# Decoder kernel with four attentions: a second bank for part of the causal stage's key projection, and GpSimd's stacking of head pairs cut in two around an addition

## Chip, cores and metric

One core of one Trainium2 chip. The metric is the device time of one execution in microseconds (us); of several executions the median is given.

## What is computed

A post-norm decoder of two layers on x of 4 x 512 x 512, float32. Each of six blocks is added to its input and layer-normalised:

```python
x = _layernorm(x + _L0_attn_ref(x, ...), axis=-1)        # rope attention, 4 heads of 128
x = _layernorm(x + _L0_xattn_ref(x, ctx, ctx, gamma))    # 8 heads over channels, below
x = _layernorm(x + _L0_ffn_ref(x, ...), axis=-1)         # ternary weights, Hadamard
x = _layernorm(x + _L1_attn_ref(x, ...), axis=-1)        # causal, 16 heads of 32, below
x = _layernorm(x + _L1_xattn_ref(x, ctx, mask), axis=-1)
x = _layernorm(x + _L1_ffn_ref(x, ...), axis=-1)         # 4-bit weights
# _L0_xattn: q, k, v are reshaped to (B, 8, 64, 512)
qk = jnp.einsum('bhdq,bhdl->bhql', qh, kh) * scale
ret = gamma * jnp.einsum('bhql,bhdl->bhdq', softmax(qk), vh)
# _L1_attn
kqv = (x @ Wqkv + bqkv).reshape(b, s, 3, 16, 32)
scores = jnp.einsum('bsnh,btnh->bnst', k, q) / math.sqrt(32)   # then masked to be causal
out = jnp.einsum('bnkq,bknh->bqnh', softmax(scores), v).reshape(b, s, 512) @ Wo + bo
```

Products that need more than one pass of float32r are split: each operand is kept as a high part and the rest, a low part, and the products high x high, high x low and low x high are summed.

## The kernel before

The program is written by hand, engine by engine. Each stage is a function (`head_attention` is the second, `causal_attention` the fourth) with one block per engine; the order inside a block is fixed by loops, and semaphores tie the blocks together. PSUM has eight banks of 128 x 512 float32, and all stages share them by number.

**Second attention** (`head_attention`, L708 on). The work is 16 groups g, one for two heads (a pair) of one batch, each of 8 tiles k (two heads, four tiles of queries). On TensorE a step makes the scores of a tile (L911, two matmuls, banks 0 to 2), transposes the probabilities of the tile three steps back (L80), and at k = 4 and 6 works off the previous group: values (L941), and at k = 6 also the inverse sums spread over partitions (L955). VectorE takes the maximum of each tile (L860), ScalarE the exponential (L829). At k = 1 of group g + 2 VectorE scales the output of group g (L880).

The operands of the scores are stacked by `HeadPairs`. SyncE loads a group's x and context into one of two slots (`load`), once the stack that used the slot is done. GpSimd then runs `stack` (L693): high part of the context (L696), scaled x (L697), high part of x (L699), then low part of the context (L701) and the low part of x (L704), which counts `stacked`. TensorE waits for `stacked` before the first scores of a group, so before k = 0. GpSimd's loop is

```python
for g in range(PAIRS):
    if g + 2 < PAIRS:
        stack(g + 2)          # waits scores_ready of group g first
    if g == 0:
        past.norm.root(pool, B - 1)
    norm.root(pool, 0, g - 2)
    add(g)                    # waits scaled (L880 of group g), adds into X (L800)
```

so the addition of group g stands behind the stack of group g + 2 and before that of group g + 3. `past.norm.root` (L164) belongs to the first attention's last batch; `norm.root` (L197, L199) to this stage's.

**Causal attention** (`causal_attention`, L1640 on). 16 groups G (four heads of one batch each; NF = 4 groups a batch) of 11 steps k. While group G's scores (L2057), transposes (L2068), values (L2088), tail (L2095) and spread (L2108) run, `project` (L2021) makes queries and keys of group G + 1: queries (j = 0) at steps 0, 0 and 1, keys (j = 1) at steps 3, 3 and 4, three passes of four matmuls each. Both use bank 6. ScalarE keeps the high part (`first.high`, L1155) and VectorE the low part (`first.low`, L1159, which counts `qk_low`) one step after the last pass. Before the first pass of the keys TensorE waits for `qk_low` of the queries, since they share the bank. Bank 7 holds the spread inverse sums (steps 7 to 8 of each group), and in some groups a transposed x, a value projection or an output.

## Time and profile before

| | |
|---|---|
| time, median of 3 runs | 1730.44 us (1727.53 to 1731.41) |
| profiled execution: its time | 1730.36 us |
| profiled execution: its span | 1728.6 us |
| TensorE busy | 1586.3 us (92%) |
| VectorE busy | 1273.3 us (74%) |
| ScalarE busy | 945.9 us (55%) |
| GpSimd busy | 734.0 us (42%) |
| second attention, on TensorE | from 259 to 482 us |
| causal attention, on TensorE | from 818 to 1260 us, about |

The profile comes from one execution. PE is TensorE's matmul side and PEld its weight load, DVE is VectorE, ACT ScalarE, POOL GpSimd, SP SyncE. L with a number is a line of the kernel; a helper's line stands for all who call it. In a timeline row stand the start and the duration in us, and in brackets how long the engine had been idle before it and what released it. Where a wait is for several semaphores the one named can be one that had long been there, and then it was another, often a transfer. The granted clock is TensorE's: 1.00 is its higher level of 2.4 GHz, 0.50 the lower of 1.2 GHz.

### The profile page before, as it was taken

What the parts mean: (1) busy time and instruction counts of PE and PEld (TensorE: products, weight loads), DVE (VectorE), ACT (ScalarE), POOL (GpSimd) and SP (SyncE); (2) the same over time, 40 slices, a digit from 0 to 9 for tenths busy, and PEclk for the clock granted to TensorE, in tenths of its full rate; (3) what the DMA queues carried; (4) which work ended last, traced back from release to release, by engine and by line L of the source; (5) the groups of instructions that cost most, each with busy time, mean ns of one, the idle gap of its engine ahead of it and who ended that gap; (6) DMA issues with size and microseconds to landing.
All of it is one profiled execution on the core that took longest, in us unless ns stands there. A gap on an engine that the chain in (4) does not pass through costs nothing. (4 is left out here: it accounts for less than half of the span.)

```text
span 1728.6 us, 26389 instructions
## 1 busy us (share of the span) xinstructions
PE 1586.3 (92%) x8780; PEld 1116.2 (65%) x8812; DVE 1273.3 (74%) x2261; ACT 945.9 (55%) x1945; POOL 734.0 (42%) x707
## 2 busy tenths in 40 slices
PE   8999998999866999998999999899898988999995
PEld 5778875566524566666667566566566766777774
DVE  6466656766878899997686684875759999767574
ACT  3222226886666676766575474663634555555642
POOL 5044164777631444534432232231233245556563
PEclk9999999999988999999999999999899999999998
DMA  6200018533020000004221121221233100000000
GB/s 219 74 1 25 1 49 214 182 118 102 23 98 1 1 1 1 1 1 125 76 74 53 55 74 38 56 74 37 88 107 94 49 1 1 1 25 25 1 25 25
DMA packets 66850, 95.73 MB, mean 55 GB/s; under 512 B 12176, under 2 KB 28688, under 8 KB 66716
## 3 DMA queue, kind: packets, MB, share of 16 engines
q1 hardware_dynamic: 60044, 81.18, 15.4%
q0 software_dynamic: 6144, 12.60, 2.8%
q8 instruction: 72, 1.18, 0.3%
q14 instruction: 62, 0.51, 0.1%
q10 hardware_dynamic: 528, 0.26, 0.1%
HBM read 56.25 MB, written 4.19 MB: 35 GB/s over the span
## 5 line engine op out<-in xcount | busy, mean ns | idle before, releaser
L2996 PE MATMUL bank<-fp_xT,fp_weights_values 128*128 128x512 f32 x704 | 187.4, 405 | 11.0 <-DVE fp_gate L2899 9.4
L1827 ACT ACTIVATE causal_probs<-bank,causal_neg 128x512 f32<-128x512 f32 (+3 forms) x256 | 134.5, 532 | 99.8 <-DVE causal_neg L1897 65.8
L2996 PEld LDWEIGHTS bank<-fp_xT,fp_weights_values 128*128 128x128 f32 x704 | 129.8, 190 | 56.6 <-DVE fp_gate L2899 17.4
L3023 PE MATMUL bank<-fp_wd,fp_hT 128*128 128x512 f32 x528 | 133.7, 394 | 4.6 <-DVE X L2921 3.5
L2908 DVE SCALAR_TENSOR_TENSOR fp_up<-bank,fp_weights_scales,fp_up 128x512 f32<-128x512 f32 x132 | 99.1, 751 | 43.9 <-ACT fp_up L2806 36.8
L860 DVE TENSOR_REDUCE heads_neg<-bank 128x1 f32<-128x512 f32 x128 | 86.5, 678 | 55.6 <-PE bank L911 55.6
L3023 PEld LDWEIGHTS bank<-fp_wd,fp_hT 128*128 128x128 f32 x528 | 98.5, 188 | 29.0 <-issue 6.6
L829 ACT ACTIVATE heads_probs<-bank,heads_neg 128x512 f32<-128x512 f32 x128 | 88.5, 696 | 42.8 <-DVE heads_neg L860 42.8
L1552 PE MATMUL bank<-weights_raw,ternary_qT 128*128 128x512 bf16 x433 | 104.7, 387 | 6.9 <-DVE ternary_z L1420 5.0
L1226 POOL TENSOR_TENSOR ternary_z<-ternary_z 128x1024 f32<-128x1024 f32 x16 | 37.7, 2357 | 165.4 <-DVE ternary_z L1420 165.4
L1167 POOL DMA_DIRECT2D causal_qS<-causal_qk x96 | 48.9, 516 | 135.3 <-DVE causal_qk L1159 135.2
L2068 PE MATMUL bank<-eye,causal_probs 128*128 128x128 f32 x640 | 100.2, 280 | 5.6 <-ACT causal_pT L1809 3.7
L355 POOL TENSOR_TENSOR rope_qk<-rope_rot 128x512 f32<-128x512 f32 x32 | 43.0, 1344 | 143.3 <-DVE rope_rot L458 141.8
L2779 POOL TENSOR_TENSOR fp_gate<-fp_gate 128x512 f32<-128x512 f32 x44 | 57.0, 1295 | 100.4 <-DVE fp_gate L2899 100.4
L2057 PE MATMUL bank<-causal_kS,causal_qS 96*128 96x512 f32 (+3 forms) x256 | 84.1, 380 | 16.9 <-ACT causal_probs L1827 13.9
L2800 ACT ACTIVATE fp_gate<-bank,fp_weights_scales 128x512 f32<-128x512 f32 x88 | 60.1, 688 | 61.5 <-PE bank L2996 55.6
L92 PE MATMUL bank<-rope_xT,rope_wT 128*128 128x512 f32 x372 | 90.2, 398 | 2.0 <-DVE rope_wT L445 2.0
L2068 PEld LDWEIGHTS bank<-eye,causal_probs 128*128 128x128 f32 x640 | 76.2, 143 | 24.1 <-issue 14.6
L2899 DVE SCALAR_TENSOR_TENSOR fp_gate<-bank,fp_weights_scales,fp_gate 128x512 f32<-128x512 f32 x88 | 63.8, 747 | 30.0 <-ACT fp_gate L2800 29.5
L92 PEld LDWEIGHTS bank<-rope_xT,rope_wT 128*128 128x128 f32 x372 | 68.9, 188 | 20.1 <-DVE rope_wT L445 4.3
L394 ACT ACTIVATE rope_qkT<-rope_qk 128x512 fp32r<-128x512 f32 x32 | 20.3, 634 | 112.2 <-POOL rope_qk L355 112.2
L1552 PEld LDWEIGHTS bank<-weights_raw,ternary_qT 128*128 128x128 bf16 x448 | 44.2, 100 | 56.6 <-DVE ternary_z L1420 7.5
(268 smaller groups left out, 4233.3 us busy)
## 6 DMA issues: line engine op xcount, KB each, us to landing
pairs_xd<-X SPq DMA_DIRECT2D x64, 128.0 KB, 2.6
pairs_cd<-in_ctx SPq DMA_DIRECT2D x64, 128.0 KB, 2.8
causal_qS<-causal_qk SPq DMA_DIRECT2D x96, 64.0 KB, 2.8
causal_qS<-causal_qk POOLq DMA_DIRECT2D x96, 64.0 KB, 2.5
causal_kS<-causal_qk SPq DMA_DIRECT2D x96, 64.0 KB, 2.9
causal_kS<-causal_qk POOLq DMA_DIRECT2D x96, 64.0 KB, 2.6
X<-in_x SPq DMA_DIRECT2D x4, 1024.0 KB, 7.9
heads_cT<-in_ctxT SPq DMA_DIRECT2D x4, 1024.0 KB, 6.0
```

Source lines behind the costliest of these rows:

```text
L92: last = pe.matmul(bank, lhs(a, k), rhs(c, k), start=n == 0, stop=n == len(steps) - 1)
L829: act.activation(probs[:, n % 4], banks[n % 3][:], ACT.Exp, bias=neg[:, g % 2, k:k + 1], accum_out=total[:, g % 2, k:k + 1]).then_inc(prob ...
L860: dve.tensor_reduce(neg[:, g % 2, k:k + 1], banks[n % 3][:], AX, ALU.max, negate=True).then_inc(neg_ready, 1)
L1552: last = pe.matmul(to[:], qT[:, t % 2, k], w[c][:, k], start=k == 0, stop=k == NF - 1)
L1827: act.activation(probs_of(i)[:, h + one], view[:, one], ACT.Exp, bias=neg[:, G % 2, at:at + 1], accum_out=total[:, G % 2, at:at + 1]).then ...
L2057: last = pe.matmul(view[:, one], qS[0:3 * DH, G % 2, h + one, i * P:(i + 1) * P], kS[0:3 * DH, G % 2, h + one, 0:(i + 1) * P], start=True, ...
L2068: last = pe.transpose(banks[3 + n % 2][:, h * P:(h + 1) * P], probs_of(i)[:, h, j * P:(j + 1) * P], ident)
L2800: act.activation(gate[:, n % 2, g // 2], banks[4 + g][:], ACT.Copy, scale=scale(n, g, 0)).then_inc(gate_even, 1)
L2899: dve.scalar_tensor_tensor(out=part, in0=banks[4 + g][:], scalar=scale(n, g, 0), in1=part, op0=ALU.mult, op1=ALU.add).then_inc(gate_odd, 1)
L2908: dve.scalar_tensor_tensor(out=up[:, n % 2], in0=banks[4 + g][:], scalar=scale(n, g, 1), in1=up[:, n % 2], op0=ALU.mult, op1=ALU.add).then ...
L2996: last = pe.matmul(banks[4 + g][:], values[:, g, n % NI, of], xT[:, part, g], start=part == 0, stop=part == 1)
L3023: last = pe.matmul(banks[t][:], hT[:, n % SLOTS, a, t * P:(t + 1) * P], wd[:, c, i], start=i == 0 and k == 0, stop=i == NI - 1 and k == 2)
```

## The change

Two parts that share no code.

1. `HeadPairs.stack` is cut into `highs` (three operations) and `lows` (two), and GpSimd's loop in the second attention becomes: `highs` of group g + 2, addition of group g - 1, `lows` of group g + 2, root. The addition is one iteration older. In the first iteration the root of the first attention's last batch stands between the halves.
2. In the causal attention the keys of a group G with G % 4 of 0 or 1 are projected into bank 7. There TensorE waits for `spread_kept` of group G - 3 instead of `qk_low` of the same group's queries. The spread of a group (L2108 before) waits for `qk_low` of all keys projected up to then.

```diff
     def stack(self, pool, g):
-        xd, cd, xS, cH, cL = (tile[:, g % 2] for tile in (self.xd, self.cd, self.xS, self.cH, self.cL))
+        self.highs(pool, g)
+        self.lows(pool, g)
+
+    def highs(self, pool, g):
+        xd, cd, xS, cH = (tile[:, g % 2] for tile in (self.xd, self.cd, self.xS, self.cH))
         pool.wait_ge(self.loaded[g % 2], 128 * (g // 2 + 1))
         pool.tensor_scalar(cH, cd, 1.0, 1.0, ALU.mult, ALU.mult).then_inc(self.high_c, 1)
         pool.tensor_scalar(xd, xd, self.SCALE, 1.0, ALU.mult, ALU.mult).then_inc(self.scaled_x, 1)
         pool.wait_ge(self.scaled_x, g + 1)
         pool.tensor_scalar(xS, xd, 1.0, 1.0, ALU.mult, ALU.mult).then_inc(self.high_x, 1)
+
+    def lows(self, pool, g):
+        xd, cd, xS, cH, cL = (tile[:, g % 2] for tile in (self.xd, self.cd, self.xS, self.cH, self.cL))
         pool.wait_ge(self.high_c, g + 1)
         pool.tensor_tensor(cL, cd, cH.bitcast(F32), ALU.subtract).then_inc(self.low_c, 1)
...
-            def stack(g):
-                pool.wait_ge(scores_ready, (g - 1) * TILES)
-                pairs.stack(pool, g)
-
...
-            for g in range(PAIRS):
+            for g in range(PAIRS + 1):
                 if g + 2 < PAIRS:
-                    stack(g + 2)
+                    pool.wait_ge(scores_ready, (g + 1) * TILES)
+                    pairs.highs(pool, g + 2)
                 if g == 0:
                     past.norm.root(pool, B - 1)
-
+                if g:
+                    add(g - 1)
+                if g + 2 < PAIRS:
+                    pairs.lows(pool, g + 2)
                 norm.root(pool, 0, g - 2)
-                add(g)
-            norm.root(pool, 0, PAIRS - 2)
...
+        def bank_of(G, j):
+            return banks[7 if j and G % NF in (1, 0) else 6]
...
-                    pe.wait_ge(qk_low, 2 * G + j)
+                    if bank_of(G, j) is banks[7]:
+                        pe.wait_ge(spread_kept, max(G - 2, 0))
+                    elif j and bank_of(G, 0) is banks[6]:
+                        pe.wait_ge(qk_low, 2 * G + j)
+                    else:
+                        pe.wait_ge(qk_low, 2 * G)
...
-                    last = pe.matmul(banks[6][:], w[a][:, k, at], xT[:, c, k], start=n == 0 and k == 0, stop=n == 2 and k == NF - 1)
+                    last = pe.matmul(bank_of(G, j)[:], w[a][:, k, at], xT[:, c, k], start=n == 0 and k == 0, stop=n == 2 and k == NF - 1)
...
             def spread_inverse(G):
                 pe.wait_ge(inverted, G + 1)
                 pe.wait_ge(spread_kept, G)
+                pe.wait_ge(qk_low, min(2 * (G + 3), 2 * GROUPS))
```

`first.high` and `first.low` read the same bank as `project` wrote. The orders of TensorE, ScalarE and VectorE stay as they were; GpSimd's changes in the second attention.

GpSimd, second attention, the addition of group 1 and the stack of group 4. Before (`pairs_` are the stacked operands, `heads_part` the scaled output, in brackets the semaphores that an instruction waits for):

```order
L800 TENSOR_TENSOR X<-heads_part,X 128x512 [waits heads_scaled,pairs_stacked]
L696 TENSOR_SCALAR pairs_cH_64<-pairs_cd_62 128x1024 [waits pairs_loaded_0,heads_scores_ready]
L697 TENSOR_SCALAR pairs_xd_61<-pairs_xd_61 128x1024
L699 TENSOR_SCALAR pairs_xS_63<-pairs_xd_61 128x1024 [waits pairs_scaled_x]
L701 TENSOR_TENSOR pairs_cL_65<-pairs_cd_62,pairs_cH_64 128x1024 [waits pairs_high_c]
L704 TENSOR_TENSOR pairs_xS_63<-pairs_xd_61,pairs_xS_63 64x1024 [waits pairs_low_c,pairs_high_x]
```

The same piece now:

```order
L700 TENSOR_SCALAR pairs_cH_64<-pairs_cd_62 128x1024 [waits pairs_loaded_0,heads_scores_ready,pairs_stacked]
L701 TENSOR_SCALAR pairs_xd_61<-pairs_xd_61 128x1024
L703 TENSOR_SCALAR pairs_xS_63<-pairs_xd_61 128x1024 [waits pairs_scaled_x]
L803 TENSOR_TENSOR X<-heads_part,X 128x512 [waits heads_scaled]
L708 TENSOR_TENSOR pairs_cL_65<-pairs_cd_62,pairs_cH_64 128x1024 [waits pairs_high_c]
L711 TENSOR_TENSOR pairs_xS_63<-pairs_xd_61,pairs_xS_63 64x1024 [waits pairs_low_c,pairs_high_x]
```

The three `TENSOR_SCALAR` rows have moved ahead of the addition; the two `TENSOR_TENSOR` rows stay behind it.

GpSimd, start of the second attention, the stack of group 2, as it is now:

```order
L700 TENSOR_SCALAR pairs_cH_64<-pairs_cd_62 128x1024 [waits pairs_loaded_0,heads_scores_ready,heads_power_set]
L701 TENSOR_SCALAR pairs_xd_61<-pairs_xd_61 128x1024
L703 TENSOR_SCALAR pairs_xS_63<-pairs_xd_61 128x1024 [waits pairs_scaled_x]
L164 TENSOR_TENSOR norm0_rstd<-norm0_var_eps,norm0_power 128x4 [waits rope_var_ready]
L708 TENSOR_TENSOR pairs_cL_65<-pairs_cd_62,pairs_cH_64 128x1024 [waits pairs_high_c]
L711 TENSOR_TENSOR pairs_xS_63<-pairs_xd_61,pairs_xS_63 64x1024 [waits pairs_low_c,pairs_high_x]
```

The root (L164) stood behind the last of these rows before, and stands in the middle now.

## Rows read from the trace of the kernel before

**Rows 1.** Waits of TensorE, second attention: line, releaser: us in total, times, longest

```profile
PE bank L911 <- POOL pairs_xS L704: 5.7, 12, 3.0
```

**Rows 2.** Waits of TensorE, causal attention, 818 to 1216 us

```profile
PE bank L2021 <- DVE causal_qk L1159: 8.4, 12, 1.5
```

**Rows 3.** Timeline of GpSimd, one group of the second attention

```profile
328.57 1.28 POOL L800 TENSOR_TENSOR X<-heads_part,X 128x512 f32<-128x512 f32 x1 [2.71 <-DVE heads_part L880]
329.94 1.05 POOL L696 TENSOR_SCALAR pairs_cH<-pairs_cd 128x1024 fp32r<-128x1024 f32 x1
...
333.14 2.38 POOL L701 TENSOR_TENSOR pairs_cL<-pairs_cd,pairs_cH 128x1024 fp32r<-128x1024 f32 x1
335.66 2.36 POOL L704 TENSOR_TENSOR pairs_xS<-pairs_xd,pairs_xS 64x1024 fp32r<-64x1024 f32 x1
...
341.70 1.28 POOL L800 TENSOR_TENSOR X<-heads_part,X 128x512 f32<-128x512 f32 x1 [2.72 <-DVE heads_part L880]
```

**Rows 4.** Timeline of TensorE, start of group 6

```profile
337.25 0.60 PE L80 MATMUL bank<-eye,heads_probs 128*128 128x128 f32 x4
338.08 0.50 PE L911 MATMUL bank<-pairs_cH,pairs_xS 128*128 128x512 f32 x1 [0.23 <-POOL pairs_xS L704]
...
338.65 0.60 PE L80 MATMUL bank<-eye,heads_probs 128*128 128x128 f32 x4
339.01 0.47 PE L911 MATMUL bank<-pairs_cH,pairs_xS 128*128 128x512 f32 x1
```

**Rows 5.** Timeline of TensorE, starts of groups 2, 4 and 15

```profile
284.45 0.50 PE L911 MATMUL bank<-pairs_cH,pairs_xS 128*128 128x512 f32 x1 [2.96 <-POOL pairs_xS L704]
...
311.80 0.50 PE L911 MATMUL bank<-pairs_cH,pairs_xS 128*128 128x512 f32 x1 [0.46 <-POOL pairs_xS L704]
...
457.99 0.50 PE L911 MATMUL bank<-pairs_cH,pairs_xS 128*128 128x512 f32 x1 [1.98 <-POOL pairs_xS L704]
```

**Rows 6.** Timeline of GpSimd, start of the stack of group 2, and the root behind it

```profile
276.40 1.05 POOL L696 TENSOR_SCALAR pairs_cH<-pairs_cd 128x1024 fp32r<-128x1024 f32 x1 [16.05 <-PE bank L911]
...
284.48 1.03 POOL L164 TENSOR_TENSOR norm_rstd<-norm_var_eps,norm_power 128x4 f32<-128x4 f32 x1
```

**Rows 7.** Timeline of VectorE, around the starts of groups 15 and 16

```profile
456.26 2.76 DVE L648 TENSOR_SCALAR weights_raw<-weights_raw,weights_rate 128x2048 f32<-128x2048 f32 x1
458.94 0.68 DVE L860 TENSOR_REDUCE heads_neg<-bank 128x1 f32<-128x512 f32 x1
...
468.97 1.28 DVE L648 TENSOR_SCALAR weights_raw<-weights_raw,weights_rate 128x2048 f32<-128x2048 f32 x1
```

**Rows 8.** Timeline of VectorE, group 6: scaling of X and the next maximum

```profile
344.86 0.55 DVE L223 TENSOR_SCALAR X<-X,norm_mean_var,norm_rstd 128x512 f32<-128x512 f32 x1
345.84 0.69 DVE L860 TENSOR_REDUCE heads_neg<-bank 128x1 f32<-128x512 f32 x1 [0.43 <-PE bank L911]
```

**Rows 9.** Timeline of TensorE, causal attention: keys of groups 1, 4 and 5

```profile
824.95 3.62 PE L2021 MATMUL bank<-causal_xT,causal_wH 128*128 128x512 f32 x8 [1.54 <-DVE causal_qk L1159]
...
900.60 2.07 PE L2021 MATMUL bank<-causal_xT,causal_wH 128*128 128x512 f32 x8 [0.73 <-DVE causal_qk L1159]
...
920.65 2.09 PE L2021 MATMUL bank<-causal_xT,causal_wH 128*128 128x512 f32 x8 [0.53 <-DVE causal_qk L1159]
```

**Rows 10.** Timeline of ScalarE: the first group's keep, and the keys' high part

```profile
833.71 0.58 ACT L1809 ACTIVATE causal_pT<-bank 128x512 f32<-128x512 f32 x1
...
904.13 0.69 ACT L1155 ACTIVATE causal_qk<-bank,causal_bias 128x512 fp32r<-128x512 f32 x1 [0.33 <-PE bank L2021]
```

**Rows 11.** Timeline of VectorE, causal attention, behind the keys of group 4

```profile
904.85 0.75 DVE L1159 SCALAR_TENSOR_TENSOR causal_qk<-bank,causal_bias,causal_qk 128x512 fp32r<-128x512 f32 x1 [0.83 <-ACT causal_qk L1155]
...
909.56 0.69 DVE L1878 COPY causal_pT<-bank 128x512 f32<-128x512 f32 x1 [0.69 <-PE bank L2068]
```

**Rows 12.** Timeline of TensorE, causal attention: a transpose of step 8 in the first group

```profile
835.11 0.60 PE L2068 MATMUL bank<-eye,causal_probs 128*128 128x128 f32 x4
```

**Rows 13.** A stretch, behind group 1's keys: PE, PEld, DVE, ACT, POOL busy, then clock, DMA share, GB/s

```profile
824.90:829.50 4.60, 4.55 (x13) 3.69 (x14) 3.23 (x8) 2.80 (x7) 3.19 (x4) 0.63 0.26 61
```

More of the change, by code:

```diff
@@ L1848, in _ @@
                 if G + 1 < GROUPS and k - late(G + 1) in (PROJECT[0][-1] + 1, PROJECT[1][-1] + 1):
-                    first.high(act, G + 1, (PROJECT[0][-1] + 1, PROJECT[1][-1] + 1).index(k - late(G + 1)), banks[6])
+                    first.high(act, G + 1, (PROJECT[0][-1] + 1, PROJECT[1][-1] + 1).index(k - late(G + 1)), bank_of(G + 1, (PROJECT[0][-1] + 1, PROJECT[1][-1] + 1).index(k - late(G + 1))))
                 for f in range(NF):
@@ L1953, in _ @@
                 if G + 1 < GROUPS and k - late(G + 1) in (PROJECT[0][-1] + 1, PROJECT[1][-1] + 1):
-                    first.low(dve, G + 1, (PROJECT[0][-1] + 1, PROJECT[1][-1] + 1).index(k - late(G + 1)), banks[6])
+                    first.low(dve, G + 1, (PROJECT[0][-1] + 1, PROJECT[1][-1] + 1).index(k - late(G + 1)), bank_of(G + 1, (PROJECT[0][-1] + 1, PROJECT[1][-1] + 1).index(k - late(G + 1))))
                 for t in range(NT):
```

## Prediction

> **What bounds the kernel now.** I first read the waits of TensorE, since it is the busiest engine, in the two stages that the change touches. In the second attention it waits for GpSimd's last stacking step, 12 times and 5.7 us in all, up to 3.0 at once [rows 1]; one more such wait lies behind that stretch [rows 5]. In the causal attention it waits 12 times and 8.4 us for the low part of a projection [rows 2]. Both are waits that the change aims its edits at, so the question is how much of each is bought, and what comes late next.
>
> Then the timeline of GpSimd over one group. The reader is to see a closed loop: the addition of group 4 starts at 328.57 and that of group 5 at 341.70, a period of 13.13, and the stack between them starts 1.37 behind the addition and ends at 335.66 + 2.36 = 338.02 [rows 3]. TensorE's first scores of the next group start at 338.08, released by that stack [rows 4]. The addition at 341.70 in turn waits 2.72 for VectorE's scaling, which stands behind the new group's first maxima [rows 3]. So each round is stack (8.1) + scores and scaling (3.6) + addition (1.4), and GpSimd sets the pace of the stage although it is busy only part of it.
>
> Then the timeline of TensorE at that place, for what a wait really costs. From the transposes at 337.25 to the scores is 0.83; one step on, with no wait, the same pair is 338.65 to 339.01, 0.36 [rows 4]. So a wait shown as 0.23 of idle costs 0.47: 0.24 more than its idle figure, because the array's tail still drains. I add 0.24 to every idle figure below.
>
> **The second attention, part by part.** No instruction is added or removed; the addition moves. The three high-part operations take 333.14 - 329.94 = 3.20 [rows 3]. They need the slot's load and the scores of the group before the last, which are done about when a group's first scores start, T. So they run from T to T + 3.2, ahead of the addition, which could not start before T + 341.70 - 338.08 = T + 3.62 anyway [rows 3, 4]. Then the addition, 1.37, and the two low-part operations, 338.02 - 333.14 = 4.88: the stack is ready at T + 9.9. TensorE comes for it at T + 13.13 - 0.47 = T + 12.66. The loop through GpSimd is then open by 2.8 us, and TensorE's own work is the bound. ScalarE's and VectorE's places against TensorE stay the same, as the exponential of the first tile follows its scores.
>
> Terms:
> - Group 2: the root moves ahead of the low parts, 1.03 [rows 6]. This stack is late already (TensorE waits 2.96 for it [rows 5]), so it is a loss: **+1.0**. Its start at 276.40 is put down to TensorE [rows 6], but the scores of group 0 were done long before, so I take that wait for the load, and it stays.
> - Group 4: 0.46 + 0.24 [rows 5]: **-0.7**.
> - Groups 5 to 14: ten waits like that at 338.08, 0.47 each [rows 4]: **-4.7**.
> - Group 15: TensorE waits 1.98 [rows 5], but VectorE is not free either. Its weight shift starts at 456.26 and takes 2.76, and the maximum of the new group's first tile follows at 458.94 [rows 7]. The same instruction takes 1.28 at 468.97 [rows 7]; the long one ends 1.08 behind the end of the stack, which released TensorE at 457.99 [rows 5]. With the stack done earlier it ends at about 457.5, so the maximum comes 1.4 earlier: **-1.4**. Not the full 2.2.
>
> The Trainium skill's page SBUF — State Buffer (SBUF: two separate sides) says that such VectorE operations and GpSimd take a shared port pair as an exclusive lock for a whole instruction. The trace agrees with it at this place; it would leave this term as it is.
>
> Sum of the second attention: -5.8. Everything behind is tied to it by semaphores and not by the clock on the wall, so I let it carry through to the end.
>
> The queues: SyncE loads a group once the stack that used the slot is done, and that is now some 3 us earlier in each group, while the high parts ask for the data some 5 us earlier. In the trace the load was the last to come only at group 2. I cost it at nothing; if that cover went, the 2.8 us of slack would go first.
>
> **The causal attention, part by part.** No instruction moves; the keys' first pass no longer waits for the queries' low part in groups 1, 4, 5, 8, 9, 12 and 13, seven of fifteen. The waits of groups 4 and 5 repeat in 8 and 9, and in 12 and 13.
> - Groups 4, 8, 12: 0.73 + 0.24 = 0.97 each [rows 9]. Does the gain survive? ScalarE's high part could start only 0.33 earlier, as that is its idle time [rows 10], and so VectorE's low part. But VectorE then waits 0.69 for TensorE at 909.56 [rows 11], and takes that too: 0.33 + 0.69 = 1.02, enough. **-2.9**.
> - Groups 5, 9, 13: 0.53 + 0.24 = 0.77 each [rows 9]; they are followed by value projections, which are TensorE's own work. **-2.3**.
> - Group 1: 1.54 + 0.24 = 1.78 [rows 9], but here ScalarE is behind: its copy at 833.71 ends at 834.3 and frees the bank of the transposes that start at 835.11 [rows 10, 12]. It catches only **-0.8**.
>
> The added wait, before the spread, is for the keys' low part. That is done at 904.85 + 0.75 = 905.60; the transposes ahead of the spread on TensorE release VectorE at 909.56 [rows 11]. It has been met 4 us before, so it costs nothing. The other wait in bank 7, for a spread two groups back, has been met too. Bounds for what comes back: nothing, if the chain of high and low parts is the bound after all; all of it, 1.78 + 2.91 + 2.31 = 7.0.
>
> Sum of the causal attention: -6.0. Both parts: -11.8, against the profiled execution's 1730.36 (0.08 from the median): **1718.5 us**.
>
> **Rivals.**
> - *The causal part is given back.* ScalarE's 0.33 [rows 10] is less than half of 0.97; if VectorE's later wait for TensorE does not yield, most is lost at the next exponentials. Left: -5.8, 1724.5. Against it: the 0.69 at 909.56 [rows 11]. Chance 0.13.
> - *The second attention's part is given back* to the next wait, ScalarE's exponentials in the first steps of a group, so that each group keeps 13.1. Left: -6.0, 1724.3. For it: ScalarE's steps are not far from TensorE's there; against: they start from the same scores. Chance 0.08.
> - *More than forecast*: group 1 takes its full 1.78 and gets its clock back. Behind that wait the granted clock is 0.63 for 4.6 us [rows 13], so 1.7 us are lost to the lower level of 1.2 GHz. With group 15's whole 2.2 that is 3.5 more: 1715.0. Chance 0.12.
> - *Slower: the low parts hold VectorE up.* They now run from T + 5.0 to T + 9.9, and VectorE's scaling of X stands at 344.86, T + 6.8, inside them [rows 8]. If it waits for a whole operation of 2.38 [rows 3] as the weight shift did [rows 7], and the maximum behind it has only 0.43 of idle [rows 8], up to 1.95 is lost in each of 13 groups: 25 us, and with the gains 1730.4 - 11.8 + 25 = 1744. It decides only if the exponential of that tile is needed on TensorE at once; its transposes come three steps later, with the values and the spread between, so most is absorbed. The skill's rule on the shared pair, on the page above, is the ground for such a hold. Chance 0.03.
> - *It does not do what it says*: the queries always stay in bank 6, so a wait for them is truly gone for keys in bank 7; little room. Chance 0.01 of no effect.
>
> **How the numbers follow.** My forecast has 0.63. The range takes in both halves' loss and the larger gain, with some 1 us of the runs' own spread at each end: 1714 to 1725.5. A measurement of this kernel tells about 0.2%, 3.5 us, from no change. Faster by more: the forecast, the larger gain and most of the two half gains, 0.91. Within: what falls short of a half gain, and no effect, 0.06. Slower: 0.03.
>
> **What would show it.** Second attention: TensorE's waits for the stack gone from group 3 on, the period of the scores 12.7 and no longer 13.1; the wait at group 2 near 4.0, with the root between the high and low parts; GpSimd's addition behind three high parts; the weight shift before group 15 at 1.3. Causal: TensorE's waits for the projection's low part down from 12 to 5, 8.4 us less 1.54 + 3 x 0.73 + 3 x 0.53, so about 3.1, and the keys' low part of group 4 only 0.3 earlier against the queries' while the copy behind it is 1.0 earlier. The forecast is wrong if the period stays at 13.1, if VectorE's scaling grows to 2 us with ScalarE late behind it, or if waits for ScalarE's exponentials grow by what the others lose.

## The result, and the profile after

The changed kernel takes 1723.08 us (median of five executions, 1720.64 to 1725.37) against 1730.44 before (also the median of five executions, not of three): ratio 0.9966, 95% interval 0.9954 to 0.9978. Timed twice more, it gave 0.9954 and 0.9960 (below). The mean of the three, 0.9960, is 6.9 us less than before, where the prediction said 11.8. The direction was right and 1723.08 lies inside the range, but the size was not right. Two single executions of later kernels, of 2599 and 4938 us, belong to a slow state and are in no ratio.

Where it was aimed, the change did what it says. A bank, here as in all rows, is one of PSUM's eight; banks 6 and 7 of the code are also called the seventh and the eighth. Waits of TensorE in the changed kernel, second attention from group 2 on (283 to 455 us), then causal attention (824 to 1226 us); line and releaser, then us in total, times, longest:

```profile
PE bank L917 <- POOL pairs_xS L711: 4.2, 1, 4.2
PE bank L917 <- ACT heads_probs L835: 0.5, 1, 0.5
```

```profile
PE bank L2037 <- DVE causal_qk L1165: 3.1, 5, 0.7
```

The eleven later waits for GpSimd's stack are gone [rows 1], and the twelve waits for a low part are five, 3.1 us as predicted [rows 2]. The waits for ScalarE's exponentials grew. The two kernels have to be compared over the same work, as the changed one runs up to 7 us ahead here: first the changed kernel from 822 to 1221 us, then the kernel before from 826 to 1228 us.

```profile
PE bank L2073 <- ACT causal_probs L1838: 13.4, 26, 1.0
```

```profile
PE bank L2057 <- ACT causal_probs L1827: 11.3, 22, 1.0
```

That is 2.1 more, against 5.3 that the keys no longer wait. Two waits behind the keys of group 1, 0.84 and 0.57 (below), are two thirds of it.

GpSimd's new order, one group of the changed kernel (timeline):

```profile
328.92 1.29 POOL L803 TENSOR_TENSOR X<-heads_part,X 128x512 f32<-128x512 f32 x1 [0.52 <-DVE heads_part L886]
...
341.56 1.28 POOL L803 TENSOR_TENSOR X<-heads_part,X 128x512 f32<-128x512 f32 x1 [0.52 <-DVE heads_part L886]
342.80 2.38 POOL L708 TENSOR_TENSOR pairs_cL<-pairs_cd,pairs_cH 128x1024 fp32r<-128x1024 f32 x1
345.32 2.38 POOL L711 TENSOR_TENSOR pairs_xS<-pairs_xd,pairs_xS 64x1024 fp32r<-64x1024 f32 x1
```

From addition to addition the period is 12.64 in place of 13.13 [rows 3], and the addition waits 0.52 for VectorE and no longer 2.7. The loop through GpSimd no longer sets the pace. Now group 2, first GpSimd, then TensorE:

```profile
276.13 1.05 POOL L700 TENSOR_SCALAR pairs_cH<-pairs_cd 128x1024 fp32r<-128x1024 f32 x1 [16.27 <-DMA pairs_cd<-in_ctx]
...
279.28 1.03 POOL L164 TENSOR_TENSOR norm_rstd<-norm_var_eps,norm_power 128x4 f32<-128x4 f32 x1
280.28 2.35 POOL L708 TENSOR_TENSOR pairs_cL<-pairs_cd,pairs_cH 128x1024 fp32r<-128x1024 f32 x1
```

```profile
285.16 0.80 PE L917 MATMUL bank<-pairs_cH,pairs_xS 128*128 128x512 f32 x1 [4.17 <-POOL pairs_xS L711]
```

The root lies between the parts as predicted, the start of the stack is released by the load (the prediction's reading of [rows 6]), and the scores take 0.80 where they took 0.50 [rows 5]: the clock is at its lower level of 1.2 GHz. The same in a table of stretches (us, TensorE busy, granted clock, DMA share, GB/s):

```profile
284.00:289.00 5.00, 3.84 (x13) 0.50 0.61 183
```

And the place ahead of group 15, where the prediction took the weight shift for the limit. VectorE, then GpSimd:

```profile
443.15 1.83 DVE L648 TENSOR_SCALAR weights_raw<-weights_raw,weights_rate 128x2048 f32<-128x2048 f32 x1
...
447.56 2.43 DVE L223 TENSOR_SCALAR X<-X,norm_mean_var,norm_rstd 128x512 f32<-128x512 f32 x1
449.91 0.68 DVE L866 TENSOR_REDUCE heads_neg<-bank 128x1 f32<-128x512 f32 x1
...
453.44 1.27 DVE L648 TENSOR_SCALAR weights_raw<-weights_raw,weights_rate 128x2048 f32<-128x2048 f32 x1
```

```profile
443.85 3.36 POOL L708 TENSOR_TENSOR pairs_cL<-pairs_cd,pairs_cH 128x1024 fp32r<-128x1024 f32 x1
447.36 2.35 POOL L711 TENSOR_TENSOR pairs_xS<-pairs_xd,pairs_xS 64x1024 fp32r<-64x1024 f32 x1
```

The long shift of [rows 7] is short now, 1.27. But the hold has moved one group earlier. The first weight shift (443.15 to 444.98) holds up the low part, 3.36 in place of 2.38. The second low part then starts 0.2 ahead of VectorE's scaling of X and holds it for its whole 2.35: the scaling takes 2.43, in the other groups 0.75. That is the mechanism of the "slower" rival, in one group and not in thirteen. The Trainium skill's page SBUF — State Buffer (SBUF: two separate sides) calls it, for some forms of VectorE operations against GpSimd's, an exclusive lock on a shared port pair, held for a whole instruction by whoever starts first; these rows agree, with either engine as the holder.

### The profile page after: what moved, and what is told of

Same layout as the page of the kernel before. It is cut to its first block and busy times, and to the rows that moved or that the text cites. A ratio compares the mean times of both kernels' runs of the same rounds, so it can differ in the third digit from the quotient of the medians.

```text
span 1723.5 us, 26425 instructions
## 1 busy us (share of the span) xinstructions
PE 1592.7 (92%) x8812; PEld 1117.3 (65%) x8812; DVE 1274.0 (74%) x2261; ACT 942.3 (55%) x1945; POOL 731.1 (42%) x707
## 5 line engine op out<-in xcount | busy, mean ns | idle before, releaser
L80 PE MATMUL bank<-eye,heads_probs 128*128 128x128 f32 x512 | 78.9, 277 | 3.4 <-DVE heads_pT L873 2.5
```

The source lines that it names most:

```text
L80: last = pe.transpose(bank[:, k * P:(k + 1) * P], source[:, k, :], ident)
```

## Experiments: each part alone

All fifteen runs are full kernels. Each expectation, on record before its run, has a theory one and a rival. For the traces I compare the start of the same TensorE instruction in two kernels; a difference that grows between two places is time lost between them. A stand is a stretch in which TensorE waits.

**GpSimd's order alone** (`order_only`).

```diff
-            return banks[7 if j and G % NF in (1, 0) else 6]
+            return banks[6]
```

with the new wait in `spread_inverse` taken out.

> Only GpSimd's new order in the second attention; all keys in the seventh bank, as before. Theory one (the places are independent, and what the trace of the change shows there is the part's own): group 2 loses 1.8 us, group 4 gains 0.7, groups 5 to 14 gain 0.5 each, group 15 gains 0.2, so 3.8 us less than before inside the stage, about 1726.6 us. Rival (the second attention's gain is given back by the phases behind it, the whole gain comes from the causal part): 1730 us, within 0.5 us of the kernel before.

Measured: ratio 0.9965 (0.9953 to 0.9978), 1723.44 against 1729.94, 6.1 us less; the interval is 3.8 to 8.1. The rival falls; theory one's 3.8 lies at the interval's edge. Its trace: groups 2 and 3 lose 1.4, group 4 gains 0.72, groups 5 to 14 gain 5.0, group 15 gains 0.20. It also shows what I had not expected: group 1 of the causal part gains 0.6 here, with its keys in the seventh bank (bank 6).

**The eighth bank alone** (`bank_only`).

```diff
-            for g in range(PAIRS + 1):
+            for g in range(PAIRS):
                 if g + 2 < PAIRS:
-                    pool.wait_ge(scores_ready, (g + 1) * TILES)
-                    pairs.highs(pool, g + 2)
+                    stack(g + 2)
...
+                add(g)
```

> Only the keys in the eighth bank in two of four groups, with the wait that guards it; GpSimd's order as before. Theory one: group 1 gains 0.6 us, each of the six later keys 0.7, about 5.0 us less than before, 1725.4 us. Rival (the causal gain is what is given back behind it): 1728 us or more. If the first two terms add up and nothing is given back, this and the run with the new order alone lie together 8.8 us under before.

Measured: 0.9982 (0.9973 to 0.9991), 1727.18 against 1729.94: 3.1 us less, 1.6 to 4.7 by the interval. Theory one's 5.0 is just outside it. The rival, 1728 or more, has its bound inside the interval, and the time does not exclude it; the trace does for the place itself, where the six later keys gain 4.38. But 5.9 are lost between 472 us and the keys of group 1, where this kernel is the kernel before (1.5 of it comes back over group 1, whose queries ran at the lower clock, 3.40 for eight products). So a part gains what its place shows, and something else takes from it elsewhere. The two parts alone add up to 9.2, the whole gave 5.9 to 8.0 in three timings; the intervals allow both. That became the second question.

## Experiments: groups 15 and 2

**The first weight shift in idle time** (`shift_idle`).

```diff
-    SHIFT_AT = ((14, 2), (14, 7), (15, 6), (16, 2))
+    SHIFT_AT = ((13, 6), (14, 7), (15, 6), (16, 2))
```

> The changed kernel with VectorE's first shift of the ternary weights at step 6 of group 13, where VectorE stands idle for 2.6 us and GpSimd has nothing to do, in place of step 2 of group 14. Theory one (group 15's gain is lost because that shift meets GpSimd's low part, which then takes 3.36 us in place of 2.4 and runs into VectorE's scaling of X, 2.43 us in place of 0.75): both durations are back to about 2.4 and 0.8, VectorE reaches group 15's end without its backlog, and the stage ends 1.2 us or a little more sooner than in the changed kernel, 1721.9 us. Rival (group 15 is set by TensorE's and ScalarE's own work, the hold is beside it): no difference over 0.2 us at group 15's start.

Measured: 0.9945 (0.9933 to 0.9958), 1720.96. Its GpSimd, then its VectorE, at the same place:

```profile
441.54 2.37 POOL L708 TENSOR_TENSOR pairs_cL<-pairs_cd,pairs_cH 128x1024 fp32r<-128x1024 f32 x1
444.05 2.37 POOL L711 TENSOR_TENSOR pairs_xS<-pairs_xd,pairs_xS 64x1024 fp32r<-64x1024 f32 x1
```

```profile
443.44 0.74 DVE L223 TENSOR_SCALAR X<-X,norm_mean_var,norm_rstd 128x512 f32<-128x512 f32 x1
```

Both holds are gone, and from group 15's start to 472 us (counted in the first profile of before) it gains 1.54 where the changed kernel gains 0.21: 1.3 regained, as theory one said. The rival falls. Its profile leads that of the changed kernel by 5.3 at the end. Of the rest, 2.1 come from groups 2 and 3, where its load landed sooner, and 1.7 from the ternary stage's end, where its clock held (below), with no edit at either; by the medians alone its 1720.96 is that of the changed kernel timed again, 1720.97. (The edit also takes 1.8 us of work out of a busy stretch of VectorE; the two are not told apart from each other, only the sum.)

**The root behind the low parts** (`root_last`).

```diff
-                if g == 0:
-                    past.norm.root(pool, B - 1)
                 if g:
                     add(g - 1)
                 if g + 2 < PAIRS:
                     pairs.lows(pool, g + 2)
+                if g == 0:
+                    past.norm.root(pool, B - 1)
```

> The changed kernel with nothing but the root of the stage before put back behind the low parts of pair 2, in GpSimd's first iteration. Theory one (of group 2's 1.8 us lost, 1.0 is the root, the rest is the lower clock behind the longer stand and a load that lands at 274.3 to 276.1 us from run to run): TensorE's wait ahead of group 2 is 1.0 us shorter than 4.17, 3.2 us or less by the landing, and the time 1.0 us under the changed kernel. Rival (the load sets group 2 alone): the wait stays over 4 us with a landing at 276.1 us.

Measured: 0.9951 (0.9938 to 0.9963), 1721.03, beside 1720.97 for the changed kernel on the same chip: theory one's 1.0 us less does not show in the time, which these runs tell to some 2 us. GpSimd and TensorE of this kernel:

```profile
275.34 1.05 POOL L700 TENSOR_SCALAR pairs_cH<-pairs_cd 128x1024 fp32r<-128x1024 f32 x1 [15.69 <-DMA pairs_cd<-in_ctx]
```

```profile
283.39 0.50 PE L917 MATMUL bank<-pairs_cH,pairs_xS 128*128 128x512 f32 x1 [2.58 <-POOL pairs_xS L711]
```

From the start of the stack to the scores are 8.05 us, against 9.03 in the changed kernel (285.16 - 276.13). So the root costs its 1.0 at this place, the wait is 2.58 and not over 4, and the landing of the load decides the rest.

**The load of pair 2 sooner, and the root behind** (`load_first`). The edit above, and on SyncE's queue:

```diff
-                if g >= 2:
+                if g > 2:
                     sp.wait_ge(pairs.stacked, g - 1)
...
                     sp.dma_start(cT[:, b % 2], rows(ctxT_in[b])).then_inc(cT_loaded[b % 2], 16)
+                if g == 1:
+                    sp.wait_ge(pairs.stacked, 1)
+                    pairs.load(sp, 2)
                 if FIRST_LOAD <= g < FIRST_LOAD + 8:
```

> The changed kernel with the load of pair 2 issued ahead of the first weights chunk on SyncE's queue, and the root of the stage before behind the low parts of pair 2. Theory one (group 2 waits for its load and then for GpSimd's 8.9 us behind it, and TensorE's stand also costs it half its clock for the next 4 us): the load lands about 3.6 us sooner, the root's 1.0 us is out of the way, TensorE's wait of 4.17 us ahead of group 2 is nearly gone (under 0.6 us), the clock stays at 1.00, and group 3 starts 4.5 to 5.5 us sooner: 1718 us. Rival (the load is set by the transfers of the stage before or by bandwidth, not by its place in the queue): the wait falls by the root's 1.0 us alone and the time by 1.0 to 1.8 us, 1721.7 us.

Measured: 0.9924 (0.9911 to 0.9936), 1717.16, 12.8 us under before. GpSimd, then TensorE at the start of group 2:

```profile
272.97 1.05 POOL L700 TENSOR_SCALAR pairs_cH<-pairs_cd 128x1024 fp32r<-128x1024 f32 x1 [12.79 <-DMA pairs_cd<-in_ctx]
```

```profile
280.73 0.60 PE L80 MATMUL bank<-eye,heads_probs 128*128 128x128 f32 x4
281.08 0.48 PE L920 MATMUL bank<-pairs_cH,pairs_xS 128*128 128x512 f32 x1
```

The load lands 3.2 us sooner, the wait is gone, the scores take 0.48, and TensorE is 5.9 us ahead of the changed kernel's profile by the end of group 3 (-3.81 against +2.08, both counted from the stage's start). The rival falls.

**That load on the kernel before** (`load_on_before`): only the lines on SyncE's queue.

> The kernel before with nothing but the load of pair 2 issued ahead of the first weights chunk. Theory one (group 2's wait is its load's, whoever orders GpSimd's work): the load lands near 272.9 us, the wait of 2.96 us is gone and with it the clock's fall, group 3 starts 3.5 to 4.5 us sooner, about 1726 us. Rival (the gain needs the changed order on GpSimd, whose parts ran 8.9 us from landing to stack with the root ahead): under 2 us.

Measured: 0.9980 (0.9970 to 0.9989), 1726.11, 3.6 us less. The load lands at 273.05, group 3 starts 4.0 sooner. The rival falls. The wait of 2.96 was the load's place in the queue and not GpSimd's order of work.

## Experiments: the causal part

**The eighth bank in one of four groups** (`bank_fourth`).

```diff
-            return banks[7 if j and G % NF in (1, 0) else 6]
+            return banks[7 if j and G % NF == 0 else 6]
```

> The changed kernel with the keys in the eighth bank in groups 4, 8 and 12 alone; in groups 1, 5, 9 and 13 they are back in the seventh. Theory one (0.71 us for each key of groups 4, 8, 12 and 0.73 for each of 5, 9, 13, nothing for group 1, whose gain of 0.6 us also shows in the kernel with the new order alone): in its trace groups 4, 8 and 12 gain 0.7 to 0.95 us, groups 5, 9, 13 nothing, and the time is 1.5 to 2.2 us over the changed kernel's. Rival (the prediction's own: group 1 gains 0.8 us too): 0.8 us more than that.

Measured: 0.9965 (0.9952 to 0.9979), 1723.61, 2.6 over the changed kernel on the same chip. In the trace groups 4, 8 and 12 gain 2.27, where all six later keys gain 4.37 in the other kernel: 0.7 to 0.76 each, whichever group. Group 1 gains 0.63 without its bank. The time alone would fit the rival, whose range was 2.3 to 3.0, better than theory one's 1.5 to 2.2; by the trace the rival falls, as the bank buys group 1 nothing here.

Where 0.97 becomes 0.71 shows in the changed kernel behind the keys of group 4. TensorE, then ScalarE:

```profile
896.85 2.11 PE L2037 MATMUL bank<-causal_xT,causal_wH 128*128 128x512 f32 x8
...
900.22 0.34 PE L2073 MATMUL bank<-causal_kS,causal_qS 96*128 96x384 f32 x1
900.61 0.63 PE L2084 MATMUL bank<-eye,causal_probs 128*128 128x128 f32 x4
901.17 2.36 PE L2104 MATMUL bank<-causal_pT,causal_v 128*32 128x512 f32 x32
```

```profile
899.20 0.69 ACT L1838 ACTIVATE causal_probs<-bank,causal_neg 128x512 f32<-128x512 f32 x1 [1.15 <-DVE causal_neg L1904]
...
899.88 0.59 ACT L1820 ACTIVATE causal_pT<-bank 128x512 f32<-128x512 f32 x1
```

The keys start with no wait. But the step behind them is slower: from the scores at 900.22 to the transposes are 0.39, in the kernel before 0.18 (903.93 to 904.11), and on to the values 0.56 in place of 0.53: 0.24 is given back within five microseconds of the keys' start. The copy that frees the transposes' bank ends at 900.47, just ahead of them; in the kernel before it ended at 903.24, 0.87 ahead. It stands on ScalarE behind an exponential that has itself waited 1.15 for VectorE. By these times it is the copy that is late first; no run moved it.

For group 1, the changed kernel's TensorE:

```profile
825.07 0.44 PE L2073 MATMUL bank<-causal_kS,causal_qS 96*128 96x384 f32 x1 [0.84 <-ACT causal_probs L1838]
...
826.53 0.44 PE L2073 MATMUL bank<-causal_kS,causal_qS 96*128 96x384 f32 x1 [0.57 <-ACT causal_probs L1838]
```

The keys' 1.54 [rows 9] has turned into 0.84 and 0.57 for ScalarE's exponentials.

## Experiments: what is given back elsewhere

**Both kernels again** (`changed_again`, `before_again`, `changed_third`: no edit).

> The changed kernel once more, unedited. Theory one (the shares are additive: stage sums of -3.8 to -4.9 us and -4.4 us from the traces; the 3 to 4 us given back behind them differ from execution to execution, as short stands of TensorE in the attention's tail, in the ternary stage's end and in the memory stage do or do not cost it its clock): the median lies between 1720 and 1724 us, and in its profile some of those places give back and others not. Rival (the give-back is systematic, part of the change): 1723 us again, and the same three places lose the same time.

> The kernel before once more, unedited: which of its short stands cost it the clock. Theory one (whether TensorE's clock falls behind the stands of 1.3 us ahead of the ternary stage's last down projection and of 3.2 us in the memory stage differs from execution to execution, with the change and without): at least one of the two places that kept a clock of 1.00 in the first profile of before falls here, or one of those that fell there does not. Rival (the change causes these falls): both places keep 1.00 as in the first profile, 12 products in 3.1 us behind the stand of 3.2 us.

> The changed kernel a third time, unedited. Theory one: 1720.5 to 1723.5 us; the load of pair 2 lands between 274.3 and 276.2 us, and the stage's gain by group 15 is 3.8 to 5.9 us as it lands; the causal groups gain 4.4 us again, to 0.1 us. Rival (the change's gain is as uncertain as the clock's places): the causal groups' gain differs by over 0.5 us.

Measured: the changed kernel 0.9954 (0.9942 to 0.9967), 1720.97, and 0.9960 (0.9948 to 0.9973), 1721.67; the kernel before against itself 1.0005 (0.9996 to 1.0014). Both medians lie where theory one put them. The causal gain of groups 2 to 15 repeats to 0.1 us (4.40, 4.37, 4.32). The gain of the second attention does not stay in its forecast range in the third profile: 6.8 by group 15 and not 3.8 to 5.9. What also does not repeat is the clock. The same products behind the same wait in the memory stage, in the first profile of before and in two of the changed kernel:

```profile
1324.66 3.07 PE L92 MATMUL bank<-memory_values,memory_pT 128*128 128x512 f32 x12 [3.22 <-DVE memory_pT L2501]
```

```profile
1318.56 5.49 PE L92 MATMUL bank<-memory_values,memory_pT 128*128 128x512 f32 x12 [3.21 <-DVE memory_pT L2518]
```

```profile
1314.62 3.06 PE L92 MATMUL bank<-memory_values,memory_pT 128*128 128x512 f32 x12 [3.20 <-DVE memory_pT L2518]
```

The stand of 3.2 us before it is the same. Over the first two of these rows the granted clock is (TensorE busy, clock, DMA share, GB/s):

```profile
1324.60:1327.70 3.10, 3.04 (x13) 1.00 0.65 184
```

```profile
1318.50:1324.00 5.50, 5.44 (x13) 0.50 0.37 106
```

At this place the lower clock costs 2.4 us. It does not stay 2.4: in every profile with 5.49 the loss has gone back to 1.1 or 1.2 by 1500 us, and in the four with 4.4 to 4.6 to 0.2 or less, since places behind it give time back. The expectation for the second run of before held by one place: behind the stand of 1.34 us in the ternary stage's end, four transposes that took 0.66 in the first profile took 1.11:

```profile
787.42 1.11 PE L1572 MATMUL bank<-eye,ternary_z 128*128 128x128 f32 x4 [1.34 <-ACT ternary_zT L1340]
```

The fall goes on through the products behind them, in the first profile of before and in that of the changed kernel:

```profile
789.05 3.62 PE L1596 MATMUL bank<-ternary_w_down,ternary_yT 128*128 128x512 bf16 x15
```

```profile
785.63 4.69 PE L1602 MATMUL bank<-ternary_w_down,ternary_yT 128*128 128x512 bf16 x15
```

This loss, 1.6 us, is whole still at 818 us. With both kernels losing at other places from profile to profile, the rival of `changed_again`, the same losses at the same places, falls: it lost 4.2 ahead of the causal part and nothing behind 1226 us, the first profile 2.2 and 2.2 (table below).

The Trainium skill's page TensorE: Matmul & The Clock Gate (Part 1: The HAM clock gate) says that the number of matmuls at the lower clock at a kernel's start varies between runs of one kernel; these rows show such a difference in the middle of one.

**Four more profiles**: `before_look1` to `before_look3` and `changed_look`, no edit.

> The kernel before, unedited, for its clock behind the stands of 1.3 us (ternary stage's end) and 3.2 us (memory stage). Theory one (whether the clock falls there is chance in both kernels): of the three looks at before at least one shows the memory stage's 12 products at 4.2 us or more in place of 3.1. Rival (the kernel before keeps its clock there, the changed one as a rule does not, so the change gives back 1 to 2 us there): 3.1 us in all three.

> The same as the look before, with the same two expectations: 4.2 us or more in at least one of three by theory one, 3.1 us in all three by the rival.

> The same once more. Its group 1 of the causal part also shows whether the keys' products behind their wait of 1.54 us run at the lower clock (3.6 us) as in the first profile or at full clock (2.1 us); by theory one both occur and the first is the rarer.

> The changed kernel, unedited: the causal groups gain 4.3 to 4.4 us against either profile of before, whatever the clock does elsewhere; the memory stage's 12 products take 4.2 us or more (rival) or either (theory one).

Measured: 1729.60, 1730.67 and 1730.74 against 1720.46. The twelve products took 3.07, 5.49 and 3.06 in the three of before and 4.56 in the changed kernel, whose causal groups gained 4.31 as expected. The second of before:

```profile
1324.03 5.49 PE L92 MATMUL bank<-memory_values,memory_pT 128*128 128x512 f32 x12 [3.20 <-DVE memory_pT L2501]
```

So the kernel before loses its clock there too, and theory one stands as it was written. But not equally often: one of five profiles of before, three of four of the changed kernel, and, with all edited kernels, ten of twelve. What that does to the sum is small, since half of it or more comes back (below). The keys of group 1 in the causal part ran at the lower clock (3.6 us, as in [rows 9]) in three of the five profiles of before, and at full clock in two:

```profile
825.50 2.09 PE L2021 MATMUL bank<-causal_xT,causal_wH 128*128 128x512 f32 x8 [1.53 <-DVE causal_qk L1159]
```

Those two gain the same 0.6 over group 1 that all edited kernels but `bank_only` gain (its queries just ahead ran at the lower clock, and it gains nothing). My expectation called the lower clock the rarer case there; in before it is the more frequent.

With nine profiles of the two kernels the change can be summed by place. Start of TensorE's instructions against the first profile of before, mean of four profiles of the changed kernel less mean of five of before (us):

| place | before, each | changed, each | difference | predicted |
|---|---|---|---|---|
| up to the second attention | 0 to -0.9 | -0.5 to -0.9 | -0.1 | 0 |
| groups 2 and 3 | 0, -1.2, +0.3, -1.5, +1.3 | +2.1, +1.1, -1.0, -1.3 | +0.4 | +1.0 |
| group 4 | 0 | -0.7 each | -0.7 | -0.7 |
| groups 5 to 14 | 0 to -0.1 | -5.0 each | -4.9 | -4.7 |
| from group 15 to 472 us | 0, +0.6, 0, +0.6, 0 | -0.2 each | -0.4 | -1.4 |
| tail, ternary stage, start of causal | 0, +1.7, +0.1, +1.7, 0 | +2.2, +4.2, +1.5, +0.7 | +1.4 | 0 |
| causal group 1 | 0, -0.6, 0, -0.6, 0 | -0.6 each | -0.4 | -0.8 |
| causal groups 2 to 15 | 0 to +0.2 | -4.4, -4.4, -4.3, -4.3 | -4.4 | -5.2 |
| behind 1226 us | 0, -0.3, -0.2, +1.0, -0.3 | +2.2, -0.2, +0.7, +2.3 | +1.2 | 0 |
| sum | | | -7.9 | -11.8 |

(The rows are rounded; the means themselves sum to -7.8.) The mean spans differ by 7.8 too: 1728.5 for the five, 1720.7 for the four. The sum agrees with the timed ratios, 5.9 to 8.0 us.

The two rows in which nothing was edited and time is lost, the tail with the ternary stage, and all behind 1226 us, can be narrowed down in the same profiles (us lost):

| stretch of the first profile | before, each | changed, each | other kernels with a key in bank 7 (six) | `order_only`, `load_on_before` |
|---|---|---|---|---|
| 785.5 to 795, ternary stage's end | 0, 1.6, 0, 1.6, 0 | 1.7, 2.9, 1.6, 0 | 3.0, 1.3, 0, 1.6, 0, 0 | 1.6, 0 |
| 1226 to 1260, last causal group | -0.1 to 0.1 | 1.1, 0, 1.0, 0.9 | 0.7 to 1.2 | 0.2, -0.1 |
| 1260 to 1300, memory stage's start | -0.1 to 0 | 0, 0, 0, 1.6 | 1.6, 1.6, 0, 0, 0, 0 | 0, 0 |
| 1300 to 1500, with the twelve products | 0, -0.1, 0, 1.1, -0.1 | 1.1, 0.1, -0.2, 0.1 | 0.2, 0.2, 1.1, 1.1, 0, 1.1 | 1.2, 1.9 |

In the last two columns the order is `bank_only`, `bank_fourth`, `shift_idle`, `root_last`, `load_first`, `all_three`, then the two named. `load_on_before` has its 1.9 mostly from a place near 1410 us that was not followed up. Of the difference of 1.4 the first stretch holds 0.9; 0.3 lie in the second attention's tail and 0.3 from 700 us on, most of it one longer wait for ScalarE in one profile. Of the 1.2 the second holds 0.7, the third 0.4 (one profile), and the fourth, with the twelve products, 0.1. The second stretch is the one that does not look like chance: nine of the ten profiles with keys in bank 7 lose 0.7 us or more there and none of the seven others does, though no key is projected there any more. It is the clock again, behind a stand of 2.22 that both kernels have. Twelve transposes and then the granted clock over 6.5 us from them, in the first profile of before and of the changed kernel:

```profile
1247.72 2.59 PE L2068 MATMUL bank<-eye,causal_probs 128*128 128x128 f32 x12 [1.96 <-ACT causal_pT L1809]
```

```profile
1241.10 2.95 PE L2084 MATMUL bank<-eye,causal_probs 128*128 128x128 f32 x12 [1.76 <-ACT causal_pT L1820]
```

```profile
1247.70:1254.20 6.50, 6.39 (x49) 0.74 0.02 4
```

```profile
1241.10:1247.60 6.50, 6.41 (x48) 0.65 0.01 4
```

Why it falls longer there with the second bank is not shown by any run.

## All three edits together

**Load, root and shift** (`all_three`), the edits of `load_first` and `shift_idle` in one kernel.

> The changed kernel with the earlier load of pair 2, the root behind the low parts and VectorE's first shift in group 13, all at once. Theory one (the places are independent): the 5.5 to 6 us of the earlier load and the 1.3 to 2.1 us of the shift add up, 7 to 8 us under the changed kernel, 1714 to 1716 us. Rival (what comes sooner is taken up by the stage's tail and the weights it loads, which wait for something else): not under 1717 us, the time of the earlier load alone.

Measured: 0.9922 (0.9909 to 0.9934), 1716.32, 13.4 us under before and 4.65 under the changed kernel on the same chip. It is faster than the kernel before and the changed kernel, just over theory one's 1714 to 1716 and short of its 7 to 8 us; the rival, not under 1717, falls by the median. Against the earlier load alone (0.9924) the two timings, on different chips, cannot be told apart. In the traces it gains the shift's 1.3 by 472 us, is 0.8 ahead at 1200 us and 0.8 behind at the end; 0.4 of that swing lies in the last causal group and 1.1 behind its twelve products in the memory stage, which took 5.49 us against 3.06. So the load's gain stands, and whether the shift is worth anything on top of it stays open.

## Why the prediction was right and wrong

- **The loop through GpSimd, right.** The period fell from 13.13 to 12.64, 0.49 a group against a predicted 0.47; group 4 gave 0.7 as predicted. The 0.24 added to each idle figure was needed: by idle figures alone the ten groups would be worth 2.3, and they gave 4.9.
- **Group 2, right in kind.** The root costs 1.0 (9.03 against 8.05 from stack to scores). What the prediction did not have is the size of the chance at this place: one execution to the next it moves by up to 2.8 us in the kernel before and 3.3 in the changed one, with the landing of one load and with the clock behind the wait.
- **Group 15, wrong: predicted -1.4, measured -0.4**, and -0.2 against the profile that the prediction was made from. The failed step is "with the stack done earlier it ends at about 457.5, so the maximum comes 1.4 earlier". It shortened one instruction and took the work ahead of it on VectorE as unchanged. The low parts now meet the first weight shift a group earlier, and VectorE pays 1.7 in its scaling of X. `shift_idle` gives 1.3 back.
- **Causal groups 4, 8, 12, mis-sized: 0.97 each predicted, 0.71 measured.** The sum "0.33 + 0.69 = 1.02, enough" looked at VectorE's low part; by the timelines ScalarE's copy ahead of the transposes was late first and took 0.24. Groups 5, 9 and 13 gave 0.73 for 0.77.
- **Causal group 1, wrong: -0.8 predicted, -0.4 measured, and that not the wait.** The failed step is that ScalarE lets 0.8 of the wait be caught up. With the clock held the bank buys nothing there: `order_only` and `bank_fourth` have the keys in bank 6 and the same gain of 0.6, and the changed kernel waits 0.84 and 0.57 for ScalarE's exponentials instead. The gain shows only against profiles in which the lower clock fell on those keys, three of five; hence -0.4 in the means. With bank 6 it fell on them in three of eight profiles, with bank 7 in none of nine; whether the bank has a part in that is open.
- **The largest miss, 2.6 of 4.0 us, and the step that failed first: "everything behind is tied to it by semaphores and not by the clock on the wall, so I let it carry through to the end".** Semaphores do carry it, but TensorE's clock behind short stands is not tied to them, and the sum had no term for it. In the unedited places the changed kernel lost 1.4 and 1.2 us more than the kernel before: 0.9 in the ternary stage's end, 0.7 in the last causal group, 0.4 at the memory stage's start. In all three the same products run longer at a lower granted clock; in the third it is one profile, `changed_look`, in which twelve products behind a stand of 1.92 took 3.98 with the clock at 0.69 around them, against 3.01 at 1.00. The memory stage's twelve products, the most striking case at 2.4 us, give only 0.1 of the difference. In the ternary stage five and four profiles, with both cases in each kernel, leave room for chance. In the last causal group they hardly do: the loss goes with the keys in bank 7, nine of ten against none of seven. Why is open; a shift of the work against whatever sets the clock would do it, and no run here separates that from another effect of the edit.
- **The rivals.** Neither part was given back whole. The "slower" rival's hold is real and happened once: in the other groups the scaling took 0.75, 0.2 longer than before. The exponentials' waits, one of the signs of being wrong, grew by 2.1 where the keys' waits fell by 5.3, most of it in group 1.

## What to carry to other kernels

Price a removed wait at its place, then look on the same engines for the next instruction that would be late within some microseconds: here 0.24 of 0.97 went that way. When an order on GpSimd moves, list the VectorE instructions that it will newly lie beside, in the irregular groups above all, since the regular ones tell nothing of them. And count a gain far upstream of short stands of TensorE as uncertain by what each fall of the clock costs, however exactly the place itself repeats. Price such a fall by what is left of it some hundred us on, and not by the products that it slows: here 2.4 us at the place were 1.1 or nothing later, while 1.6 us elsewhere stayed. Sums of waits are to be taken over the same work, and not over the same microseconds.

## What the runs showed of the hardware

- One and the same stand of 3.2 us cost TensorE's following twelve products nothing (3.06 us, granted clock 1.00) or 2.4 us (5.49, granted clock 0.50), in the same kernel on different executions. Of the 2.4 us 1.1 was left 180 us later.
- A granted clock below 1.00 followed a stand of 2.22 us in all 17 profiles, and stands of 1.34, 1.54 and 3.2 us in some of them only.
- A VectorE operation of 0.54 us took 2.43 beside a GpSimd operation of 2.35 that had started 0.2 ahead, and a GpSimd operation of 2.38 took 3.36 beside a VectorE one that had started 0.7 ahead.
- A load of 1 MB in eight transfers, issued behind 2 MB of others on the same queue, landed between 274.2 and 276.4 us in the nine profiles of the two kernels; issued ahead of one of those megabytes it landed at 271.4, 273.0 and 273.1 in three others (by the start of the stack that it releases).
